# Evacuating LayerNorm transposes in one piece, and PV matmuls one slot later, in a fused attention and FFN layer on eight cores

## The reference

```python
x: (4, 4096, 1024) float32
h   = LN(x) * ln_gamma + ln_beta
qkv = h @ w_qkv + b_qkv                  # 16 heads of 64
a   = softmax(q k^T / 8) v               # per batch and head, 4096 x 4096
y   = x + a @ w_out + b_out
x1  = LN(x + y)
s = x1 @ Win + bin_;  h = relu(s[..., None] * W1 + b1)   # 64 x 16
g = einsum(h, W2) + b2;  f = g @ Wout + bout
out = LN(x1 + f)
```

## Time and profile before

| | us |
|---|---|
| median of 3 runs | 2166.51 (2165.51 to 2166.72) |
| the profiled execution | 2164.13 |
| its span, core 7 (the slowest) | 2162.6 |
| spans of the 8 cores | 2151.8 to 2162.6 |
| PE busy in the span | 1477.5 (68%) |
| DVE busy | 607.8 (28%) |
| ACT busy | 1360.2 (63%) |
| granted TensorE clock, mean of the 8 cores | 0.856 to 0.861 |

### The profile page before, as it was taken

One profiled execution on the slowest core, in us unless ns is written; L12 is line 12 of the kernel. 1 busy time (PEld: TensorE's weight loads), 2 busy tenths in 40 slices (PEclk: granted clock), 3 DMA queues, 4 the chain that ended last, 5 costly groups with the idle time before them and its releaser, 6 DMA issues. The chain is left out here.

```text
span 2162.6 us, 26829 instructions; the slowest of 8 cores (2151.8 to 2162.6 us)
## 1 busy us (share of the span) xinstructions
PE 1477.5 (68%) x8552; PEld 509.8 (24%) x8552; DVE 607.8 (28%) x806; ACT 1360.2 (63%) x1478; POOL 26.1 (1%) x35
## 2 busy tenths in 40 slices
PE   1443388868977885898689778858985665454443
PEld 0221123222322222232223222222321221122111
DVE  3333312231232223122212322231222011345555
ACT  3777277767767776777677677767776886032222
POOL 0000000000000000000000000000000000000000
PEclk9676599999999999899999999999998998666555
DMA  6222000100010001001000100010000001402102
GB/s 105 88 78 69 0 1 6 11 1 6 1 10 1 6 1 11 1 6 10 1 6 1 10 1 6 1 10 1 6 1 1 1 1 35 92 0 78 54 25 78
DMA packets 44598, 44.36 MB, mean 21 GB/s; under 512 B 34993, under 2 KB 35122, under 8 KB 44466
## 3 DMA queue, kind: packets, MB, share of 16 engines
q1 hardware_dynamic: 16162, 33.72, 5.1%
q0 software_dynamic: 28304, 8.92, 4.2%
HBM read 43.16 MB, written 8.39 MB: 24 GB/s over the span
## 5 line engine op out<-in xcount | busy, mean ns | idle before, releaser
L833 ACT ACTIVATE PT_sb<-score_ps,negB_sb 128x1024 bf16<-128x1024 f32 x1024 | 1140.9, 1114 | 331.3 <-PE score_ps L751 253.9
L749 PE MATMUL score_ps<-qT_sb,kT_sb 64*128 64x512 bf16 x1024 | 403.7, 398 | 196.6 <-ACT PT_sb L833 116.6
L765 PE MATMUL pv_ps<-PT_sb,v_sb 128*64 128x512 bf16 x1024 | 415.5, 406 | 87.8 <-DVE attnT_sb L790 74.0
L769 PE MATMUL pv_ps<-PT_sb,v_sb 128*64 128x512 bf16 x1024 | 416.4, 407 | 0.0
L751 PE MATMUL score_ps<-qT_sb,kT_sb 64*128 64x512 bf16 x1024 | 407.4, 402 | 0.0
L772 PE MATMUL z_ps<-PT_sb,onesb_sb 128*64 128x512 bf16 x1024 | 403.5, 394 | 0.0
L775 PE MATMUL z_ps<-PT_sb,onesb_sb 128*64 128x512 bf16 x1024 | 403.5, 394 | 0.0
L604 PE MATMUL qkv_ps<-xhq_sb,wq_sb 128*128 128x512 bf16 x1120 | 315.7, 408 | 10.6 <-DVE qT_sb L619 5.3
L749 PEld LDWEIGHTS score_ps<-qT_sb,kT_sb 64*128 64x128 bf16 x1024 | 94.5, 93 | 599.8 <-issue 597.4
L765 PEld LDWEIGHTS pv_ps<-PT_sb,v_sb 128*64 128x64 bf16 x1024 | 113.0, 110 | 278.8 <-issue 231.7
L787 DVE RECIPROCAL zb_sb<-z_ps 128x512 f32<-128x512 f32 x32 | 107.4, 3358 | 158.8 <-PE z_ps L775 117.3
(11 more groups left out here) (80 smaller groups left out, 829.4 us busy)
## 6 DMA issues: line engine op xcount, KB each, us to landing
xtile_sb<-x SPq DMA_DIRECT2D x32, 512.0 KB, 3.9
xres_sb<-x SPq DMA_DIRECT2D x16, 512.0 KB, 8.2
out<-u_sb SPq DMA_DIRECT2D x16, 512.0 KB, 3.8
wq_sb<-wqkv POOLq DMA_DIRECT2D x24, 256.0 KB, 6.0
wout_sb<-wout POOLq DMA_DIRECT2D x1, 2048.0 KB, 22.1
win_sb<-win POOLq DMA_DIRECT2D x1, 128.0 KB, 22.4
rw_sb<-rw POOLq DMA_DIRECT2D x1, 128.0 KB, 22.4
w2b_sb<-w2b POOLq DMA_DIRECT2D x1, 128.0 KB, 22.4
```

Source lines behind the costliest of these rows:

```text
L749: e.matmul(o, w, r, start=True, stop=True))
L765: a=s0, b=s1: e.matmul(o, w, r, start=a, stop=b, skip_group_check=True))
L769: e.matmul(o, w, r, start=a, stop=b, skip_group_check=True))
L833: e.activation(out=o, in_=i_, func=AF.Exp, bias=b, scale=0.125))
```

## The change

There are two changes in one diff.

In `phase_ln` the eight ScalarE instructions that evacuate a tile's transposes, each with gamma and beta, become one plain copy of 128x1024 without them. After every fourth tile VectorE applies gamma and beta in place to the slice of 512 rows, in eight `tensor_scalar` instructions of 128x512 in bf16. It waits for the fourth copy first. The bursts and the QKV matmuls of later head pairs wait for VectorE's counter in place of ScalarE's.

In `p2_subgroup` odd slot kt gets PV and Z of key tiles kt-3 and kt-2 where it had kt-2 and kt-1, so the first such group of a query tile stands in slot 3 and not in slot 1, and `finish_qt` issues the last two key tiles' PV and Z where it had one, after its wait for the last exponential.

```diff
--- before.py
+++ after.py
@@ -346,6 +346,7 @@
     s_evac_t = [None] * 32
     last_xh_read = [0, 0]
     last_score_evac = [0, 0]
+    v_gb_slice = [0] * 8
     last_qkv_evac = [0]
     w3_waited = [False]
 
@@ -374,7 +375,7 @@
         if pi[0] >= len(pend):
             return False
         m, n = pend[pi[0]]
-        if s_evac_t[4 * n + 3] is None:
+        if not v_gb_slice[n]:
             return False
         pi[0] += 1
         if not w3_waited[0]:
@@ -382,7 +383,8 @@
             w3_waited[0] = True
         j = {8: 0, 16: 1, 0: 2}[m]
         wbuf = wq3_sb[:, j * 1024:(j + 1) * 1024]
-        sc.wait("tensor", ss, max(s_evac_t[4 * n + 3], last_qkv_evac[0]))
+        sc.wait("tensor", sv, v_gb_slice[n])
+        sc.wait("tensor", ss, last_qkv_evac[0])
         for kc in range(8):
             last = kc == 7
             def mk(o, w, r, s0, s1, last=last):
@@ -471,23 +473,33 @@
             t_tp = st.inc()
             last_xh_read[par] = t_tp
             sc.wait("scalar", st, t_tp)
-            s_e = 0
-            for kc in range(8):
-                dst = xhq_sb[:, kc * T_FULL + i * 128:
-                             kc * T_FULL + i * 128 + 128]
-                s_e = sc.s(lambda e, o=dst, i_=sps[:, kc * 128:kc * 128 + 128],
-                           ga=gamT_sb[:, kc:kc + 1], be=betT_sb[:, kc:kc + 1]:
-                           e.activation(out=o, in_=i_, func=AF.Identity,
-                                        bias=be, scale=ga))
+            dst = xhq_sb[:].rearrange("p (kc t) -> p kc t", kc=8)[
+                :, :, i * 128:i * 128 + 128]
+            srcv = sps.rearrange("p (kc t) -> p kc t", kc=8)
+            s_e = sc.s(lambda e, o=dst, i_=srcv: e.copy(out=o, in_=i_))
             s_evac_t[i] = s_e
             last_score_evac[par] = s_e
+            if i % 4 == 3:
+                n = i // 4
+                sc.wait("vector", ss, s_e)
+                v_gb = 0
+                for kc in range(8):
+                    slc = xhq_sb[:, kc * T_FULL + n * 512:
+                                 kc * T_FULL + n * 512 + 512]
+                    v_gb = sc.v(lambda e, o=slc, i_=slc,
+                                ga=gamT_sb[:, kc:kc + 1],
+                                be=betT_sb[:, kc:kc + 1]:
+                                e.tensor_scalar(o, i_, ga, be,
+                                                op0=AluOpType.mult,
+                                                op1=AluOpType.add))
+                v_gb_slice[n] = v_gb
             qkv_burst()
     while pi[0] < len(pend) or pending_evac:
         made = qkv_evac()
         made = qkv_burst() or made
         if not made:
             break
-    L["v_gb_s"] = s_evac_t[31]
+    L["v_gb"] = v_gb_slice[7]
     state["lqe_s"] = last_qkv_evac[0]
     state["last_qkv_evac"] = 0
     state["last_tp_evac"] = 0
@@ -590,7 +602,7 @@
                 dst = qT_sb[:, qbase + n * 512:qbase + n * 512 + 512]
             sc.wait("tensor", wq_ready[j][0], wq_ready[j][1])
             if first:
-                sc.wait("tensor", ss, L["v_gb_s"])
+                sc.wait("tensor", sv, L["v_gb"])
                 if sg >= 2:
                     sc.wait("vector", st, state["kv_parity_free"][par])
                 first = False
@@ -778,7 +790,8 @@
 
     def finish_qt(h, pqt, hit):
         sc.wait("tensor", ss, h["exp_done"][NKT - 1])
-        h["pvz_done"][NKT - 1] = emit_pvz(pqt, NKT - 1, hit, h["exp_done"])
+        for j in (NKT - 2, NKT - 1):
+            h["pvz_done"][j] = emit_pvz(pqt, j, hit, h["exp_done"])
         if gen is not None:
             next(gen, None)
             next(gen, None)
@@ -814,10 +827,9 @@
                 sc_done.append(emit_scores(qt, kt + 1, gg))
             else:
                 sc.wait("tensor", ss, exp_done[kt - 1])
-            if kt % 2 == 1:
-                if kt >= 2:
-                    pvz_done[kt - 2] = emit_pvz(qt, kt - 2, it, exp_done)
-                pvz_done[kt - 1] = emit_pvz(qt, kt - 1, it, exp_done)
+            if kt % 2 == 1 and kt >= 3:
+                pvz_done[kt - 3] = emit_pvz(qt, kt - 3, it, exp_done)
+                pvz_done[kt - 2] = emit_pvz(qt, kt - 2, it, exp_done)
             spar = kt % 4
             pt = PT_sb[:, spar * 1024:spar * 1024 + 1024]
             g1 = sc_done[kt]
```

## The result

The kernel after takes 2078.3 us, the median of 9 runs (before 2166.0 in the runs beside them). The ratio of the times is 0.959 (0.958 to 0.960): 4.1% faster. The forecast was 2077 us.

A forecast was written before the change was run, and what follows sets the result against it. ScalarE was taken to bound the LN stage, and attention's exponentials to wait for TensorE's scores. 2164.1 - 48 - 75 - 5 + 3.5 + 35 = 2074.6, with the median 2.4 us higher: 2077 us, own range 2050 to 2105.

The forecast's parts named there:

- the sum: Whole kernel: 2164.1 - 48 - 75 - 5 + 3.5 + 35 = 2074.6 us, for the profiled execution.
- the LN stage: Stage before attention: gamma and beta move to VectorE, last slice ready at 181.6 us; gain 48 us.
- (a): Query tile boundaries in attention: scores no longer behind the PV that waits for the division; 3.6 x 21 = 75 us gained.
- the branch that the sum took: Query tile boundaries: TensorE's gap of 1.1 us leaves the clock at 1.0, so a boundary gains 3.85 us, not 2.6.
- (c): Mid-tile in attention: exponentials wait for a later-freed PT buffer, 7.60 us per QKV tile instead of 7.24; 35 us lost.
- (b): Head pair ends: nothing hides the 0.43 us of the extra key tile's PV; 8 x 0.43 = 3.5 us lost.
- (a) in the last head pair: Three query tile boundaries without a next head pair's work between: 1.8 x 3 = 5 us gained.
- (4): Rival, attention: slower, the new PT buffer wait falls at the half clock and starves ScalarE; 2235 us, chance 0.05.
- (1): Rival, attention: no net gain, boundaries at 2.6 us each against mid-tile and pair-end losses; 2118 us, chance 0.20.
- (2): Rival, LN stage: keeps a bound near the old one (0.75 us instructions, half clock), gain 22; 2103 us, chance 0.12.
- (5): Rival, both stages: nothing moves because both waits were covered; 2166 us, chance 0.02.
- (3): Rival, mid-tile in attention: the PT buffer wait doesn't bite; 2042 us, chance 0.08.

The follow-up runs named there:

- e8: The kernel after with constants 1.0 and 0.0 in place of the gamma and beta operands in VectorE's tensor_scalar; 2069.7 us, ratio to before 0.956.
- e5: The kernel after with five PT buffers and PV of key tiles 0, 1, 2 in slot 3, then kt-2 and kt-1; 2041.2 us, ratio to before 0.942.
- e3: The kernel after with five PT buffers instead of four; 2037.9 us, ratio to before 0.942.
- e4: The kernel after, four PT buffers, with PV of key tiles 0, 1, 2 in slot 3, then kt-2 and kt-1; 2041.8 us, ratio to before 0.944.
- e9: The kernel after with five PT buffers, four x buffers and the gamma and beta scaling one tile later on VectorE; 2013.1 us, ratio to before 0.929.

## Why the prediction was right

The time is within 1.3 us of the forecast, and part of that closeness is luck. Against the sum, the LN stage gave 0.8 us less and attention 3.4 less (38.1 where the sum has 75 + 5 - 3.5 - 35 = 41.5), and 0.6 came from behind attention. So the span came out 3.6 us above the sum (2076.7, where 2162.6 - 48 - 41.5 is 2073.1). What hid 2.3 of these is that the runs' median lay 3.9 us above the profiled span before (2166.5 and 2162.6), and lies only 1.6 above it after.

**The LN stage: right in mechanism and size.** Forecast 48 us; 47.2 measured at the first exponential, in an execution whose first load landed 2.4 us later than before (26.81 against 24.37). The burst behind the last slice was put near 182 and starts at 182.41; the copy at 1.05 us and takes 1.01; the tensor_scalar at 0.42 and takes 0.413. That the row nearest in type and width (L649, 0.42) gave the right number is luck in part: with two constants the instruction is faster than that row (0.29, e8), and its two per-partition operands add about what that gains. The waits of VectorE stand where the prediction laid them, for the fourth copy (2.60, forecast 2.4) and for one load (1.44), and the seven periods take 134.2 us for a forecast of 137.7 - 2.7 = 135.0. Inside that sum two small terms were off: the four slices with three bursts were put at 20.1 us and the others at 19.1, and measured they are 19.3, 20.7, 18.9 and 18.9, then 19.4 and 19.4. The Trainium skill (VectorE: DVE Perf Modes, the perf-mode tier table) gives an estimate of 0.29 us for this instruction. The trace of e8 agrees, with constants; with two per-partition operands the measurement is 0.413 and decides.

**(a) The boundaries: right.** Exp(4) was to wait for PV(0) and come 0.82 us behind it; it comes 0.78 behind. TensorE's longest idle was to fall to 1.1 us and is 1.05, and the clock stays at 1.00 with it in 20 of 21 boundaries, the branch that the sum took. Where it fell, query tile 3 of head pair 2 takes 63.1 us where 61.6 to 61.9 is usual. PV's wait for the division, forecast near 30 us, is 28.6. From the table, with (c) at its measured 0.32 a QKV tile and (b) at 0.43 taken out, the three boundaries of a head pair gave 2.66 + 1.28 = 3.9, 2.88 + 1.28 = 4.2, and 2.04 + 0.32 + 0.43 = 2.8: together 10.9, for 3 x 3.6 = 10.8. Two slips in the prediction's working change nothing in the sum: scores(2) was ahead of PV(0) already (1105.60 and 1108.91), so only scores(3) and (4) stood behind it, and 21 boundaries at 2.6 us are 55 us, not 56.

**(a) in the last head pair: mis-sized.** 1.8 us were forecast for each of its three boundaries. Exp(4) comes 0.82 us behind PV(0), as laid out, but the sum took it that no exponential behind it is late, and at a clock of 0.50 two are. Order of time and windows of the kernel after there:

```profile
1617.48 0.37 PE L761 MATMUL score_ps<-qT_sb,kT_sb 64*128 64x512 bf16 x1 [0.91 <-ACT PT_sb L845]
1618.69 0.37 PE L761 MATMUL score_ps<-qT_sb,kT_sb 64*128 64x512 bf16 x1 [0.81 <-ACT PT_sb L845]
...
1620.17 0.38 PE L777 MATMUL pv_ps<-PT_sb,v_sb 128*64 128x512 bf16 x1 [1.09 <-DVE attnT_sb L803]
...
1620.99 1.11 ACT L845 ACTIVATE PT_sb<-score_ps,negB_sb 128x1024 bf16<-128x1024 f32 x1 [1.24 <-PE z_ps L787]
...
1624.01 3.53 ACT L845 ACTIVATE PT_sb<-score_ps,negB_sb 128x1024 bf16<-128x1024 f32 x3 [0.51 <-PE z_ps L787]
```

```profile
1618.00:1620.00 2.00, 0.39 (x2) 0.12 (x2) 1.90 (x2) 1.66 (x2) 0.00 (x0) 1.00 0.00 0
...
1621.00:1623.00 2.00, 1.98 (x10) 0.42 (x8) 0.00 (x0) 1.72 (x2) 0.00 (x0) 0.50 0.00 0
```

With no next head pair's matmuls to fill it, TensorE does one pair of scores between gaps of 0.91, 0.81 and 1.09 us, and the clock falls to 0.50. Two more exponentials are late for it (0.28 in between, and 0.51). The three boundaries gain 0.9, 1.4 and 1.4 us and the pair's first tile loses 0.4, so the pair gains 3.2 us, not 5. Its steady part has no gap, as forecast: 26 exponentials in a row.

```profile
1706.80 31.28 ACT L845 ACTIVATE PT_sb<-score_ps,negB_sb 128x1024 bf16<-128x1024 f32 x26 [0.51 <-PE z_ps L787]
```

**(b) right:** e5 against e3 has 0.4 us at a pair's end, where 0.43 was forecast.

**(c) right in mechanism, slightly off in size.** 7.56 us a QKV tile for a forecast 7.60: 98 x 0.32 = 31 us, not 35. The wait and its place are shown by e3 and e4. What the prediction missed is the start of a head pair. Order of time in the kernel after, head pair 1, and a window:

```profile
418.55 0.58 PE L761 MATMUL score_ps<-qT_sb,kT_sb 64*128 64x512 bf16 x1 [5.96 <-ACT PT_sb L845]
...
423.88 1.11 ACT L845 ACTIVATE PT_sb<-score_ps,negB_sb 128x1024 bf16<-128x1024 f32 x1 [1.85 <-PE z_ps L787]
```

```profile
420.00:422.00 2.00, 2.00 (x6) 0.44 (x4) 0.00 (x0) 1.91 (x2) 0.00 (x0) 0.50 0.00 0
```

TensorE comes out of the softmax bound's steps at the half clock, and there exp(4) waits 1.85 us for Z. In the kernel before, exp(4) of head pairs 1 to 6 is 0.71 to 1.00 us late. Tile 0 takes 2.1 us more than before, where 5 x 0.32 = 1.6 are the QKV tiles; the other 0.5 a pair falls at this place. It looks like the wait of rival (4), confined to one place in each pair, but e3 shows that the buffer is not all of it: there no exponential waits for `z_ps`, and tile 0 still takes 0.8 us more than before (41.0 for 40.2), with exp(5) of head pair 1 waiting 1.01 us for scores(5). In both kernels PV of two key tiles stands in slot 3, ahead of scores(5), at the half clock. No run changed that by itself, so the cause of this 0.5 us stays open.

By head pair attention gains 4.0, 4.8, 3.9, 5.2, 5.4, 5.2, 6.3 and 3.2 us, 38.1 in all. Head pairs 0 and 2 hold most of what the terms above leave over: the stalls of pair 0 were shorter before (its tiles 1 and 2 took 45.2 and 46.4 us, not 46.2 and 47.7), and in pair 2 the clock fell once.

**The rivals.** (1) and (4) fall with the clock of 0.97 in attention and the boundaries' 10.9 us. (2) falls with 0.413 us and 182.41. (5) falls with both stages shorter. (3) falls with the two gaps in six exponentials; its 2042 us is what the kernel takes once that wait is taken away, 2041.8 in e4 and 2037.9 in e3.

Open: the spread of tile 0 from one head pair to the next in the same execution (in e5 from 40.8 to 42.2 us) was not followed up. A version of e9 in which the bursts of TensorE run at full clock in the LN stage was not tried, nor one in which the division is made shorter, though PV(0) still waits 1.05 us for it.

## What to carry over

A consumer that is moved later also frees its buffer later: before moving it, lay out which producer waits for that buffer, and compare the new loop with each kind of turn, not with their mean (2.40 us hid under 2.60, but not under 2.04). Then try one more buffer: here it was worth 40 us where the whole change was worth 88. When a bound moves to another engine, look in its order of work for the waits that the engine before had covered, for a copy and for a load here, and take both away: with the one for the copy gone alone, the one for the load grew from 1.7 to 2.0 us a slice.

## What was not expected of the hardware

- Per-partition operands cost time on VectorE: tensor_scalar 128x512 bf16 to bf16 in SBUF takes 0.29 us with two constants and 0.413 us with two `[128, 1]` operands (e8 against the kernel after), 0.12 us for the pair of them.
- The clock fell to 0.50 in the last head pair behind three gaps of at most 1.09 us, with one pair of matmuls of 0.37 us between each. At a boundary with a single gap of 1.05 us among more matmuls it stayed at 1.00. At the one boundary of head pair 2 where it fell, the longest gap is also 1.05 us. The longest single gap alone, by which the prediction went, does not tell these places apart. The Trainium skill (TensorE: Matmul & The Clock Gate, Part 1) says that the gate halves the clock after TensorE has idled. The rows don't contradict it, and no run here shows how several short gaps count together.
